# Windowed attention in 32-row pieces: a block transpose on VectorE for the turned probabilities, and roots seeded by ScalarE

## The reference

```
h = x with its upper 64 channels shifted by one token
q, k, v = split(h @ Wqkv)                     # 16 heads of 64
q, k = q / |q|, k / |k|, then rotated by cos and sin tables
for each window of 32 tokens: keys are the window before and the window itself (64)
    p = softmax(8 q k^T, masked);  out = p @ v
x = x + out @ Wo
xn = (x - mean) / sqrt(var + 1e-5)
x = x + ((xn W1a + b) * gelu(xn W1g + b)) @ W2 + b2
```

## Time and profile before

| | us |
|---|---|
| runs (3) | 4609.84, 4618.05, 4621.47; median 4618.05 |
| the profiled execution | 4616.27, of which span 4614.5 |
| busy: TensorE, its weight loads | 4320.6, 2899.1 |
| busy: VectorE, GpSimd, ScalarE | 2891.1, 2746.8, 2273.4 |
| mean granted TensorE clock | 0.938 |

### The profile page before, as it was taken

One profiled execution on the slowest core, in us unless ns is written; L12 is line 12 of the kernel. 1 busy time (PEld: TensorE's weight loads), 2 busy tenths in 40 slices (PEclk: granted clock), 3 DMA queues, 4 the chain that ended last, 5 costly groups with the idle time before them and its releaser, 6 DMA issues. The chain is left out here.

```text
span 4614.5 us, 133631 instructions
## 1 busy us (share of the span) xinstructions
PE 4320.6 (94%) x57968; PEld 2899.1 (63%) x57968; DVE 2891.1 (63%) x3838; ACT 2273.4 (49%) x2592; POOL 2746.8 (60%) x3511
## 2 busy tenths in 40 slices
PE   8999889999999999999967876999999999999997
PEld 3333357676766776767736663676767667677674
DVE  1575167767767677777634335677776776767773
ACT  2454245555555555555521112555555565555553
POOL 0000077777777777777604114877777777777772
PEclk9899989999999999999976557999999999999998
DMA  0000000000000000000000001000000000000000
GB/s 17 1 1 1 23 34 11 11 16 11 2 17 11 16 11 2 7 2 2 2 7 4 4 4 56 11 11 2 16 11 16 12 2 16 11 7 2 2 2 10
DMA packets 14134, 46.53 MB, mean 10 GB/s; under 512 B 3808, under 2 KB 6240, under 8 KB 11744
## 3 DMA queue, kind: packets, MB, share of 16 engines
q1 hardware_dynamic: 13536, 37.83, 2.4%
HBM read 36.78 MB, written 1.05 MB: 8 GB/s over the span
## 5 line engine op out<-in xcount | busy, mean ns | idle before, releaser
L718 POOL TENSOR_TENSOR w_qk<-w_turned 128x1024 f32<-128x1024 f32 x384 | 904.4, 2355 | 119.0 <-DVE w_turned L601 89.6
L596 DVE TENSOR_TENSOR w_turned<-w_ps_qk,w_rot_l 128x1024 f32<-128x1024 f32 x384 | 469.9, 1224 | 719.7 <-ACT w_squares L498 700.0
L255 PE MATMUL w_ps_qk<-w_w_qk,ZT 128*128 128x512 f32 x1536 | 751.7, 613 | 37.1 <-DVE w_turned L601 18.2
L305 PE MATMUL w_ps_y<-w_px,w_w_vo 128*128 128x128 f32 x6144 | 752.5, 276 | 7.0 <-ACT w_px L502 6.7
L305 PEld LDWEIGHTS w_ps_y<-w_px,w_w_vo 128*128 128x128 f32 x6144 | 722.5, 193 | 31.8 <-issue 21.0
L747 POOL TENSOR_TENSOR w_qk<-w_qk,w_inv_norm 128x1024 f32<-128x1024 f32 x384 | 722.8, 1904 | 0.0
L498 ACT ACTIVATE w_squares<-w_ps_qk 128x1024 f32<-128x1024 f32 x384 | 391.3, 1019 | 436.5 <-PE w_ps_qk L255 436.1
L601 DVE TENSOR_TENSOR w_turned<-w_ps_qk,w_rot_l 128x1024 f32<-128x1024 f32 x384 | 466.5, 1215 | 0.0
L605 DVE TENSOR_REDUCE w_sumsq<-w_squares 128x16 f32<-128x1024 f32 x384 | 455.4, 1186 | 0.0
L502 ACT ACTIVATE w_px<-w_ps_t 128x1024 f32<-128x1024 f32 x192 | 196.5, 1024 | 509.7 <-PE w_ps_t L297 509.7
L255 PEld LDWEIGHTS w_ps_qk<-w_w_qk,ZT 128*128 128x128 f32 x1536 | 266.7, 194 | 266.7 <-issue 240.9
(11 more groups left out here) (254 smaller groups left out, 7349.5 us busy)
## 6 DMA issues: line engine op xcount, KB each, us to landing
w_w_qk<-in_w_qk SPq DMA_DIRECT2D x12, 1024.0 KB, 4.9
w_w_vT<-in_w_vT SPq DMA_DIRECT2D x12, 512.0 KB, 3.7
w_w_o<-in_w_o SPq DMA_DIRECT2D x12, 512.0 KB, 4.7
w_w<-in_w SPq DMA_DIRECT2D x12, 384.0 KB, 3.1
w_w<-in_w SPq DMA_DIRECT2D x12, 192.0 KB, 3.1
XT<-in_x SPq DMA_DIRECT2D x1, 1024.0 KB, 4.8
w_rot<-in_rot SPq DMA_DIRECT2D x2, 512.0 KB, 5.9
out<-XT SPq DMA_DIRECT2D x1, 1024.0 KB, 3.9
```

Of the source, the lines that this page charges most:

```text
L255: last = nc.tensor.matmul(ps_qk[:, c, :], Z[:, T.col:T.col + P], w_qk[:, T.parity, cols], start=True, stop=True)
L305: last = nc.tensor.matmul(ps_y[:, D.t * P:(D.t + 1) * P].rearrange("p (a v q) -> p a v q", a=2, q=WIN), w_vo[:, D.parity, h, p, :], px[:, ...
L596: nc.vector.tensor_tensor(turned[:, which, 0, :].rearrange("p (h d) -> p h d", d=DH), flat(ps_qk[:]).rearrange("p (h d) -> p h d", d=DH), ...
L718: nc.gpsimd.tensor_tensor(qk[:, T.odd, which, :], turned[:, which, 0, :], turned[:, which, 1, :], ALU.add).then_inc(pool_add, 1)
```

## The change

- The tokens are transposed at two offsets instead of four (and none at the edge of a batch). `x_tok` holds, for each tile, the tokens of the window before and of the window itself.
- The probabilities are no longer turned by TensorE and copied by ScalarE: VectorE's 32 x 32 block transpose writes `pT` from `probs` in SBUF.
- `gather` is one call of eight products of 32 rows and 512 columns, four row groups twice, into four banks (`ps_w`, which ps_t and ps_s are now parts of), accumulating. `px` has a buffer for odd and one for even tiles, and `output` reads it a step later.
- The guess of the inverse roots is ScalarE's square root and VectorE's reciprocal, and one Newton step is left of three. Behind the root ScalarE runs an exp of one column.
- The order of the steps changes on all four engines: centring and the first gate or up come ahead of the second projection, one or two pairs of `output` behind the gather, exp of the probabilities after the first squares, row sum ahead of the first rotation, maximum and subtraction behind the floor of the squares, y at VectorE's end, and on GpSimd the scaling of the probabilities ahead of the first add.

Cut to its core:

```diff
--- before.py
+++ after.py
...
-ROOT_BITS, NEWTONS = 0x5F3759DF, 3
+NEWTONS = 1
...
-        bits = sb("bits", [P, NORMS], I32)
+        root, guess, warm_in = sb("root", [P, NORMS]), sb("guess", [P, NORMS]), sb("warm_in", [P, 1])
...
-        x_win = sb("x_win", [P, TILES * WINS + 2, DIM])
+        x_tok = sb("x_tok", [P, TILES, 2, DIM])
...
-        pT = sb("pT", [P, PAIRS, P])
-        px = sb("px", [P, 2, 2, 2, PAIRS, WIN])
+        pT = sb("pT", [P, 2, HEADS, WIN])
+        px = sb("px", [P, 2, WINS, HEADS, WIN])
+        warm = sb("warm", [P, 1])
...
-        ps_t = ps("ps_t", [P, 2, 512])
-        ps_s = ps("ps_s", [P, 2, 512])
+        ps_w = ps("ps_w", [P, 4, 512])
+        ps_t, ps_s = ps_w[:, 0:2, :], ps_w[:, 2:4, :]
...
-            def windows(B, at, count, done):
-                for w in range(count):
-                    last = nc.tensor.transpose(ps_f[:, w * P:(w + 1) * P], Z[:, at + w * WIN:at + w * WIN + P], ident[:])
-                last.then_inc(done, 1)
+            def tokens(B):
+                for half in range(2):
+                    at = B.col - WIN * (1 - half)
+                    last = nc.tensor.transpose(ps_f[:, half * P:(half + 1) * P], Z[:, at:at + P], ident[:])
+                last.then_inc(pe_xt, 1)
...
-            def turn_probs(C):
-                for p in range(PAIRS):
-                    last = nc.tensor.transpose(ps_t[:, p // 4, (p % 4) * P:(p % 4 + 1) * P],
-                                               probs[:, 2 * p:2 * p + 2, :].rearrange("p h k -> p (h k)"), ident[:])
-                last.then_inc(pe_pt, 1)
...
-            def gather(C, half, bank):
-                for v in range(2):
-                    w = 2 * half + v
-                    for h in range(2):
-                        rows = slice(h * KEYS, (h + 1) * KEYS)
-                        last = nc.tensor.matmul(
-                            bank[:, h, v * 256:(v + 1) * 256].rearrange("p (a q) -> p a q", q=WIN),
-                            x_win[rows, slot(C, w, h), :], pT[rows, :, w * WIN:(w + 1) * WIN], start=True, stop=True)
+            def gather(C):
+                for half in range(2):
+                    for w in range(WINS):
+                        rows = slice(w * WIN, (w + 1) * WIN)
+                        last = nc.tensor.matmul(ps_w[:, w, :], x_tok[rows, C.t, half, :],
+                                                pT[rows, half].rearrange("p h q -> p (h q)"),
+                                                start=half == 0, stop=half == 1)
                 last.then_inc(pe_px, 1)
...
                 elif s.B and s.k % TILES:
+                    if s.k % TILES == 1 and s.C:
+                        pe.wait_ge(act_xt, s.C.n + 1)
                     if s.gate:
                         pe.wait_ge(dve_xn, s.gate.m + 1)
+                    elif s.bc:
+                        pe.wait_ge(dve_var, s.bc.m + 1)
+                    elif s.up:
+                        pe.wait_ge(act_gate, s.up.m * FFB + FFB)
...
-                    tokens(s)
+                    elif s.k == 3:
+                        pe.wait_ge(dve_bias, L0 + 1)
+                    tokens(s.B)
...
+                elif s.bc:
+                    broadcast(s)
...
+            def place_3(s):
+                if s.B and s.k % TILES == 0:
+                    if s.cen:
+                        pe.wait_ge(dve_var, s.cen.m + 1)
+                    tokens(s.B)
+                if s.bc and s.merge():
+                    layer, parity, quarters = s.merge()
+                    pe.wait_ge(act_m, layer * 4 + quarters[1] + 1)
+                    broadcast(s)
...
-                if D:
-                    if C:
-                        pe.wait_ge(dve_sub, C.n + 1)
-                    gather(D, 1, ps_s)
...
-                    output(D, range(PAIRS // 2))
+                    output(D, range(5))
                 if B:
                     pe.wait_ge(pool_qk, B.n * 2 + 2)
                     pe.wait_ge(act_tq, B.n + 1)
                     turn(B, 1, pe_tk)
+                last_pairs = 7 if s.gate or s.up else 6
                 if D:
-                    output(D, range(PAIRS // 2, PAIRS)).then_inc(pe_y, 1)
+                    output(D, range(5, last_pairs))
+                place_1(s)
                 if T:
                     pe.wait_ge(dve_turn, T.n * 2 + 1)
                     project(T, 1, pe_k)
-                place_1(s)
                 if C:
                     if B:
                         pe.wait_ge(act_tk, B.n + 1)
-                    pe.wait_ge(pool_p, C.n + 1)
-                    turn_probs(C)
+                    pe.wait_ge(dve_sub, C.n + 1)
+                    pe.wait_ge(dve_pt, C.n + 1)
+                    pe.wait_ge(act_xt, C.n + 1)
+                    gather(C)
                 place_2(s)
+                if D:
+                    output(D, range(last_pairs, PAIRS)).then_inc(pe_y, 1)
                 if B:
                     pe.wait_ge(act_tk, B.n + 1)
-                    if D:
-                        pe.wait_ge(act_px, D.n * 2 + 2)
-                    elif C:
-                        pe.wait_ge(dve_sub, C.n + 1)
+                    if C:
+                        pe.wait_ge(act_px, C.n * 2 + 1)
                     scores(B)
                 place_3(s)
-                if C:
-                    pe.wait_ge(act_pt, C.n + 1)
-                    pe.wait_ge(act_xt, C.n + 1)
-                    gather(C, 0, ps_t)
-                place_4(s)
...
-            def gathered(C, half, bank):
-                act.wait_ge(pe_px, C.n * 2 + half + 1)
-                nc.scalar.activation(px[:, half].rearrange("p h v a q -> p (h v a q)"), flat(bank[:]),
+            def gathered(C, half):
+                pair = slice(2 - 2 * half, 4 - 2 * half)
+                nc.scalar.activation(px[:, C.odd, pair].rearrange("p w h q -> p (w h q)"), flat(ps_w[:, pair, :]),
                                      ACT.Copy).then_inc(act_px, 1)
...
-            def tokens_out(B, C):
+            def tokens_out(B):
                 act.wait_ge(pe_xt, B.n + 1)
-                nc.scalar.activation(flat(x_win[:, WINS * B.t:WINS * (B.t + 1), :]), ps_f[:], ACT.Copy).then_inc(act_xt, 1)
+                nc.scalar.activation(flat(x_tok[:, B.t]), ps_f[:, 0:2 * P], ACT.Copy).then_inc(act_xt, 1)
...
-                if D:
-                    gathered(D, 1, ps_s)
+                if C:
+                    act.wait_ge(dve_sub, C.n + 1)
+                    nc.scalar.activation(probs[:], probs[:], ACT.Exp).then_inc(act_exp, 1)
...
-                if T:
-                    square(T, 1, pe_k)
...
                     gate(s.gate, 0)
+                if T:
+                    square(T, 1, pe_k)
                 if C:
-                    act.wait_ge(pe_pt, C.n + 1)
-                    nc.scalar.activation(flat(pT[:]), flat(ps_t[:]), ACT.Copy).then_inc(act_pt, 1)
+                    act.wait_ge(pe_px, C.n + 1)
+                    if D and D.k:
+                        act.wait_ge(pe_y, D.n)
+                    gathered(C, 0)
                 if s.merge():
                     merged(layer, parity, quarters[1])
                 if s.gate:
                     gate(s.gate, 1)
+                if C:
+                    gathered(C, 1)
+                if s.gate:
                     gate(s.gate, 2)
-                if C:
-                    if D:
-                        act.wait_ge(pe_y, D.n + 1)
-                    gathered(C, 0, ps_t)
                 if B and s.k % TILES == 0:
-                    tokens_out(B, C)
-                if s.edge:
-                    act.wait_ge(pe_xe, s.edge.batch + 1)
-                    nc.scalar.activation(flat(x_win[:, TILES * WINS:TILES * WINS + 2, :]), ps_f[:, 0:2 * P],
-                                         ACT.Copy).then_inc(act_xe, 1)
-                if B:
-                    act.wait_ge(dve_sub, B.n + 1)
-                    nc.scalar.activation(probs[:], probs[:], ACT.Exp).then_inc(act_exp, 1)
-
+                    tokens_out(B)
+                if s.chain is not None:
+                    act.wait_ge(dve_floor, s.chain + 1)
+                    if s.k:
+                        act.wait_ge(dve_guess, s.chain)
+                    nc.scalar.activation(root[:], sumsq[:], ACT.Sqrt).then_inc(act_root, 1)
+                if s.chain is not None or s.up:
+                    nc.scalar.activation(warm[:], warm_in[:], ACT.Exp)
+
...
-                if T:
-                    if T.k % PER == 0:
-                        dve.wait_ge(pool_rot, T.layer + 1)
-                    rotate(T, 0)
...
-                    sum_squares(T, 0)
+                    if T.k % PER == 0:
+                        dve.wait_ge(pool_rot, T.layer + 1)
+                    rotate(T, 0)
...
-                if s.y:
-                    f = s.y
...
+                if C:
+                    dve.wait_ge(pool_p, C.n + 1)
+                    if D:
+                        dve.wait_ge(pe_px, D.n + 1)
```

(50 more changed lines are left out.)

101 lines of the change are left out of this document (35 added, 66 removed).

## The result

The changed kernel takes 4693.98 us (median of 4 runs, 4684.57 to 4700.74); the kernel before, measured beside it, 4619.76 (4609.84 to 4626.79). The ratio is 1.0159, with a 95% interval from 1.0140 to 1.0179: **slower by 1.6%, where I forecast faster** (4555, range 4400 to 4690; the median lies 4 us above its end). The profiled execution took 4700.74, its span 4698.9.

What follows compares the result with a forecast made beforehand. TensorE was taken to bound both windowed stages; its 265 us saved would nearly all become waiting on a ring through ScalarE's root, leaving gains of 44 and 15 us: 4616.3 - 59 = 4557, stated as 4555, range 4400 to 4690.

Steps and rivals of the forecast that it cites:

- the ring: Second projection P, squares, root, exp, row sum, reciprocal, rotation, next P: never under 14.8 us, longer where ScalarE reaches root late.
- 0 to 1: From P of step 0 to P of step 1 (k mod 4): root behind tokens, 17.4 us; TensorE alone 14.3 to 15.4.
- 2 to 3: From P of step 2 to P of step 3: root behind the third gate, 18.0 us; TensorE alone 15.9.
- 0.4 for the floor: Short VectorE operation on the sum of squares, ahead of the root: 0.4 us, estimated from a short operation's 0.25.
- Sum 70.4, against 4 x 17.83 = 71.3: Four P-to-P steps, forecast against the profiled step: gain 0.23 us a step, 44 us over 192.
- the walk: Following the ring's operations in order from P to P: 17.4, 16.4, 18.0, 18.5 us; 4490 to 4604 as it stands, chance 0.48.
- gain some 1 us each, 15 in all: The seven steps a run ahead of the feed-forward, without gate or down, gain some 1 us each, 15 in all.
- The clock: Rival: clock falls to 1.2 GHz in TensorE's new gaps; once in four steps costs 82 us, 4637; chance 0.24.
- The transpose at twice its time: Rival: VectorE's block transpose with strided output takes 2.5 us, not 1.25; 96 us more, 4651; chance 0.07.
- The longer table switch: Rival: each table switch holds ScalarE for twice its load; 317 us more, 4872; chance 0.03.
- The serial gather: Rival: gather's row groups run one after another; 4.8 us more a step, over 5400 in the end; chance 0.01.
- TensorE-bound: Rival: TensorE stays the bound, its saved 265 us come out whole: 4350; half the gain 4480; together chance 0.17.

Runs made afterwards that it cites:

- e2: The changed kernel without both short VectorE operations (halved, floor) ahead of the maximum, their work moved to ScalarE's root and GpSimd's Newton step; 4640.38 us, 1.0042 against the kernel before.
- e12: The changed kernel without the two short VectorE operations, root ahead of third gate and token copies, third hidden product ahead of the subtraction; 4490.78 us, 0.9718 against the kernel before.
- e6: New attention with the old seed (no root), its four short VectorE operations moved from ahead of the maximum to directly behind it; 4565.12 us, 0.9873 against the kernel before.
- e4: New attention with the old seed (no root), its four short VectorE operations behind the subtraction; 4641.47 us, 1.0060 against the kernel before.
- e8: The changed kernel with the root, with its waits, ahead of the third gate and token copies on ScalarE; 4567.38 us, 0.9907 against the kernel before.

## Why the prediction was wrong

**What held.** The bound of the old kernel; the sizes of the gather (1206.65 to 1208.58, 1.93 a step against 1.9), transpose, root and load; that the busy work saved on TensorE turns into waiting; and the ring with its root behind tokens and third gate. In e2, where nothing short meets the add, the medians read 17.32, 16.72, 17.94, 18.67 against 17.4, 16.4, 18.0, 18.5. The changed kernel itself is near them too in 0 to 1 (17.23) and 2 to 3 (17.79).

**The 139 us by parts** (4 steps, 48 rounds):

- *"0.4 for the floor"*: the step of the prediction that failed. I took a short operation's duration from a place where GpSimd's add was over, and moved it to one where the add runs. It measured 1.31 + 0.17, and maximum, subtraction, reciprocal and hidden product behind it came late. By the removal of both short operations (e2) it is worth 54 us.
- *"Sum 70.4, against 4 x 17.83 = 71.3"*: a walk without any irregularity was set against a mean that holds them. The medians of before sum to 70.5, so the walk promised a gain of 0.1 a round, not 0.9: 38 us that were never there. Not all of what a mean holds is irregular: before, the steps 1 to 2 with a merge and no gap average 17.68, those without a merge 16.38, and the walk gave a merge 0.25.
- *No term for instruction supply.* Means stand 0.74 above medians a round before and 1.37 after; the difference, 0.63 x 48, is 30 us. That the gaps make it is read from the steps, not shown by an experiment: in the middle of both stages the 28 steps of the changed kernel with a gap in their score products are 39.7 us over the medians of their kinds, together; before, 10 steps are 11.0 us over. Where a gap falls in a step 1, which now hangs on scores, maximum, subtraction and tokens, P comes late by up to the whole gap.
- *"gain some 1 us each, 15 in all"* for the steps ahead of the feed-forward: the first twelve took 206.0 and 201.8 us in the two runs of the changed kernel, and 201.6 and 200.3 in the kernel before. They lost 6 instead: 21 us. Here too the lock is at work: in e2 the first seven steps of the two runs take 9 us less than in the changed kernel, and these 9 are in the 54 already.

Together 143, or 134 without what is counted twice, against 139. These are estimates that overlap at their edges, and the trace is of the slowest of the four runs, so the near sum proves little. The lock alone would have left the forecast at 4609, inside its range and still below the kernel before: it took the other terms to turn the sign. The chances failed in one respect more: three of my rivals asked what the new operations cost, none what an old one costs in a new place.

**The rivals.** The clock did fall, though nowhere near once in four steps. In the middle of the two stages the changed kernel has six stretches at 1.2 GHz, of 3.4 to 6.8 us and 24 us together, where the kernel before has one. One of them, behind a gap of 3.54 us (columns as in the earlier trace rows):

```profile
1362.60:1366.00 3.40, 3.40 (x6) 1.25 (x6) 1.09 (x2) 0.00 (x0) 0.50 (x2) 0.51 0.04 10
```

At half the clock 24 us do 12 us less of work, before 2: some 10 of the 139 us at most, a small term that the sum lacked, and partly in the means above. The transpose at twice its time: 1234 ns, not so. The longer table switch: 1283 ns, root 0.02 behind it (1195.94 + 1.28 = 1197.22, 1197.24), not so. The serial gather: 1.93 us, not so. TensorE-bound: not in the changed kernel; but e12, with both losses cured, has TensorE busy 478 of 500 us in the same window. Its 4491 is near the 4480 that I gave for half the gain, which is luck: it is another kernel, and its gain has other sources.

A rule I had at hand and didn't weigh: the Trainium skill (SBUF — State Buffer, Who interferes with whom) says that VectorE and GpSimd share a pair of ports that one holds for its whole instruction while the other blocks, and that a `tensor_scalar` can enter the modes that need it while a `tensor_reduce` on trn2 can't. The trace agrees in both: the `tensor_scalar` ended 0.04 us behind the add in 192 of 192 steps, and the 144 sums of squares, each a reduction, that began during an add took no longer than the others.

## What to carry to other kernels

Before a short VectorE operation that reads and writes SBUF is moved, look at what GpSimd does at the new place: it may cost the rest of GpSimd's instruction. Moving it one long operation further back, to where that instruction is over, can free it (e6), and moving it too far can cost more than the lock (e4). An operation on which a ring through several engines hangs should stand on its own engine ahead of copies that can wait: one root moved past two copies was worth 127 us here, more than the change had cost. And when a walk of the profile is set against a measured step, take the median step of the same kind, and give what the mean holds beyond it a term of its own.

## What the hardware showed that I had not expected

- A 36-element operation can take 1.9 us: it is held by another engine's instruction, and its duration, not the idle time ahead of it, carries the wait. A view of waits doesn't show it; the line's min/median/max (182/1314/1887) does.
- TensorE can run out of instructions. That is my reading; what the traces show is this. 128 score products are 256 instructions, one packet's worth, issued in 1.5 us. In the changed kernel all 33 gaps end 2.2 to 3.2 us after the start of a 16 KB instruction packet that began from 0.42 us ahead of the burst's start to 0.50 behind it. A packet starts that near to 52 of the 192 bursts: 33 of these have a gap, and none of the other 140. Which steps are hit depends mostly on the place of their code within 16 KB. The score products are not the only ones: 12 more gaps over 0.6 us that no engine ended stand before other products of the two stages (9 end 2.2 to 2.9 us after a packet's start), and in the kernel before 7 (all of them do).
- A table load begins ahead of its operation's wait (e8: load at 1175.64, operation released by VectorE at 1177.19), so it is free where the engine would wait anyway.
